# A two-layer transformer on one core: part products for layer 1's projections, and layer 2's scores as paired float32r products in bursts

## What is computed

```
x = x + attn0(layernorm(x));  x = x + ffn0(layernorm(x))
x = x + attn1(layernorm(x));  x = x + ffn1(layernorm(x))

attn0: q = (x @ w_q.T) in 16 heads;  k = x @ w_k.T;  v = x @ w_v.T     (one k and v for all heads)
       softmax(q k^T * softmax_scale) v, then @ w_out.T
ffn0:  x and the kernel rounded to fp8, product in float32, times the scales, to bfloat16, plus bias
attn1: q, k, v of all 16 heads from w_in;  scores = q k^T / 4 + slope_h * (key - query), -inf above the diagonal
       softmax, times v, then @ w_out.T
ffn1:  x @ W.T + b + x @ (up_aux @ lora_up @ lora_down @ down_aux).T
```

## Time and profile before

| | us |
|---|---|
| timed, median of 3 (lowest, highest) | 3888.25 (3883.73, 3889.77) |
| the profiled execution's own time | 3863.94 |
| its span | 3862.2 |
| PE busy in the span | 3636.8 (94%) |
| DVE busy | 2936.6 (76%) |
| ACT busy | 2471.1 (64%) |
| POOL busy | 1717.7 (44%) |

### The profile page before, as it was taken

One profiled execution on the slowest core, in us unless ns is written; L12 is line 12 of the kernel. 1 busy time (PEld: TensorE's weight loads), 2 busy tenths in 40 slices (PEclk: granted clock), 3 DMA queues, 4 the chain that ended last, 5 costly groups with the idle time before them and its releaser, 6 DMA issues. The chain is left out here.

```text
span 3862.2 us, 76074 instructions
## 1 busy us (share of the span) xinstructions
PE 3636.8 (94%) x25352; PEld 1854.5 (48%) x25352; DVE 2936.6 (76%) x8436; ACT 2471.1 (64%) x5347; POOL 1717.7 (44%) x1956
## 2 busy tenths in 40 slices
PE   5999999999999999998289999999999999999997
PEld 2344444444444444444145555555555555555554
DVE  4899999989998999995076776777767767777664
ACT  2777777777787777776055555555555555555554
POOL 1255555554555555554433343442433434424331
PEclk7999999999999999999599999999999999999999
DMA  3334333333333333331375755756657557566570
GB/s 70 73 77 87 80 90 76 83 79 91 76 82 88 85 84 81 83 74 37 72 120 89 127 104 96 122 105 105 115 93 124 106 94 125 104 103 116 94 122 23
DMA packets 323077, 352.93 MB, mean 91 GB/s; under 512 B 28101, under 2 KB 277371, under 8 KB 322683
## 3 DMA queue, kind: packets, MB, share of 16 engines
q1 hardware_dynamic: 320641, 347.01, 47.6%
q10 hardware_dynamic: 2048, 1.05, 0.1%
HBM read 221.08 MB, written 117.44 MB: 88 GB/s over the span
## 5 line engine op out<-in xcount | busy, mean ns | idle before, releaser
L666 DVE TENSOR_REDUCE maxima<-ps_vector 128x1 f32<-128x512 f32 x2048 | 1282.8, 682 | 162.0 <-PE ps_vector L435 155.6
L1559 DVE CUSTOM_DVE_ANT_0 ps_max<-ps_max,mask 128x128 f32<-128x128 f32 (+3 forms) x2048 | 987.2, 508 | 531.4 <-PE ps_max L1258 512.7
L1416 ACT ACTIVATE probs<-ps_exp 128x512 f32<-128x512 f32 (+3 forms) x2048 | 823.1, 441 | 783.6 <-PE ps_exp L1277 716.0
L564 ACT ACTIVATE probs<-ps_scalar 128x512 f32<-128x512 f32 x2048 | 1073.6, 604 | 155.6 <-PE ps_scalar L449 150.8
L435 PE MATMUL ps_vector<-k_op,q_op 48*128 48x512 f32 x2048 | 715.9, 446 | 48.1 <-DVE maxima L666 28.4
L449 PE MATMUL ps_scalar<-q_op,k_op 50*128 50x512 f32 x2048 | 708.1, 441 | 1.0 <-DVE o_rows L730 0.5
L1273 PE MATMUL ps_exp<-q_op,k_op 101*128 101x512 bf16 (+3 forms) x2048 | 614.3, 301 | 25.6 <-ACT probs L1416 18.0
L1258 PE MATMUL ps_max<-k_op,q_op 99*128 99x128 bf16 (+3 forms) x2048 | 619.4, 304 | 19.9 <-DMA k_op<-qk_parts 16.3
L435 PEld LDWEIGHTS ps_vector<-k_op,q_op 48*128 48x128 f32 x2048 | 333.3, 187 | 549.6 <-DVE maxima L666 394.8
L468 PE MATMUL ps_pv<-probs,v_op 128*32 128x512 f32 x4096 | 552.5, 606 | 0.0
L1704 POOL TENSOR_SCALAR neg_mean<-meanvar 128x4 f32<-128x4 f32 x64 | 12.5, 196 | 1092.0 <-issue 784.6
(11 more groups left out here) (127 smaller groups left out, 5186.0 us busy)
## 6 DMA issues: line engine op xcount, KB each, us to landing
q_op<-qk_parts SPq DMA_DIRECT2D x192, 256.0 KB, 5.9
qk_parts<-qparts SPq DMA_DIRECT2D x128, 384.0 KB, 3.2
q_op<-qk_parts SPq DMA_DIRECT2D x384, 128.0 KB, 6.4
k_op<-qk_parts SPq DMA_DIRECT2D x384, 128.0 KB, 6.9
qk_parts<-qparts SPq DMA_DIRECT2D x64, 512.0 KB, 4.2
xin<-in_x SPq DMA_DIRECT2D x32, 512.0 KB, 4.8
xres<-in_x SPq DMA_DIRECT2D x32, 512.0 KB, 4.6
x_mid<-xo SPq DMA_DIRECT2D x32, 512.0 KB, 3.2
```

What stands on the lines that cost most here:

```text
L564: act.activation(probs[:, quad % 2, at:at + S], ps_scalar[:, bank_of("scalar", "exp", p, 0, par), :], ACT.Exp).then_inc(ps_out["exp"], 1)
L666: dve.tensor_reduce(at, ps_vector[:, bank_of("vector", "max", k, d, par), :], AX.X, ALU.max).then_inc(ps_out["max"], 1)
L1416: act.activation(probs[:, quad % 2, at:at + nq], ps_exp[:, bank, 0:nq], ACT.Exp).then_inc(exp_done, 1)
L1559: ins = dve.tensor_tensor_reduce(row, row, mask[:, S - keys:S], 1.0, LOWEST, ALU.add, ALU.max, at)
```

## The change

In the first layer the projections for q, for keys with values and of the output become three products of float32r parts each, for both halves of the 256 columns (`TERMS`). The weights' parts are made once by DVE at the start. The parts of the operands are made by POOL in every body: `cut_x` twice and `cut_ont` twice, two instructions each. ACT writes the transposed columns to one staging tile first, which POOL then cuts. To fit, `xin`, `xo`, `kvf`, `kparts` and `o_rows` have one buffer instead of two. The plan is another one, and POOL and SP read their order from it too.

The second layer is written anew after the pattern of the first: q and k in two float32r parts (two POOL instructions), 51 and 53 rows high, heads 0 to 7 and 8 to 15 in the two halves of the partitions, operands in float32. Maximum tile and exponential tile of one pair have the same width, the widest first. The masks of a burst of pairs are issued ahead of it, into the banks of its exponentials (`put_mask`). The order comes from a plan, with 64 pairs in 21 bursts; three banks are for maxima and four for all the rest. A product with v waits for the tiles that it reads, not for the whole head group. The bias is added to x1 in place, and the output goes out one item after the body instead of two.

```
 PLAN_MQA = """
-PPP stat2:2:-2 qk:0:1
-PPP otr:2:-1 V
...
-PPPP otr:0:0 out:0:-1 ft:0:-2
-PPP V
-PPP split:0:1 stat1:1:2 out:1:-1
+PPP load_x:0:2 store_qk:0:1 qk:0:1
+PPP kv:0:1 split_qk:0:1
+PPP m:1:0 stat2:2:-2 split_kv:0:1 V
+PPP load_m:1:0 stat2:3:-2 norm2:0:-2 V stat1:0:2 over:0:-2 cut_ont:0:-1 V
...
+PPP ffn:0:-2 cut_x:1:2 split:0:1 otr:1:0 out:0:-1
+PPP m:0:1 load_q:1:1 load_m:0:1 V finish:0:-2 stat2:0:-1 ffn:1:-2 xt:0:2 stat2:1:-1 out:1:-1
+PPP xt:1:2 V store:0:-2
 first layer, PE's tasks:
                 elif kind == "qk":
-                    pe.wait_ge(ps_out["xt"], per["xt"] * (c + 1))
-                    for kt in range(KT):
-                        mm = pe.matmul(ps[:, :], w_qk[:, kt, k * P:(k + 1) * P], xT[:, cp, kt, :],
-                                       start=(kt == 0), stop=(kt == KT - 1))
+                    pe.wait_ge(x_cut, KT * (c + 1))
+                    for n, (kt, xp, wp) in enumerate(TERMS):
+                        mm = pe.matmul(ps[:, :], w_qk[:, wp, kt, k * P:(k + 1) * P], xT[:, xp, kt, :],
+                                       start=(n == 0), stop=(n == len(TERMS) - 1))
                 elif kind == "out":
-                    pe.wait_ge(ps_out["ont"], per["ont"] * (c + 1))
+                    pe.wait_ge(ont_cut, KT * (c + 1))
                     for t in (2 * k, 2 * k + 1):
-                        for kt in range(KT):
-                            mm = pe.matmul(ps[:, (t % 2) * D:(t % 2 + 1) * D], o_cols[:, kt, t * P:(t + 1) * P],
-                                           w_o[:, kt, :], start=(kt == 0), stop=(kt == KT - 1))
+                        for n, (kt, xp, wp) in enumerate(TERMS):
+                            mm = pe.matmul(ps[:, (t % 2) * D:(t % 2 + 1) * D], o_cols[:, xp, kt, t * P:(t + 1) * P],
+                                           w_o[:, wp, kt, :], start=(n == 0), stop=(n == len(TERMS) - 1))
 first layer, POOL:
+            def cut_x(c, k):
...
+                pool.wait_ge(ps_out["xt"], KT * c + k + 1)
+                split(x_cols[:, :], xT[:, :, k, :], x_step, KT * c + k).then_inc(x_cut, 1)
+
+            def cut_ont(c, k):
...
+                pool.wait_ge(ps_out["ont"], KT * c + k + 1)
+                split(o_half[:, :], o_cols[:, :, k, :], ont_step, KT * c + k).then_inc(ont_cut, 1)
 second layer, PE (removed and added):
-                pe.matmul(ps_max[:, bank, 0:keys], q_op[0:KA, cp * HEADS + h, i * P:(i + 1) * P],
-                          k_op[0:KA, kh, 0:keys], start=True, stop=True).then_inc(max_full, 1)
...
-                mm = pe.matmul(ps_exp[:, bank, 0:nq], k_op[0:KB, kh, T * P:(T + 1) * P],
-                               q_op[0:KB, par * HEADS + s, q0:q0 + nq], start=True, stop=not CAUSAL)
-                if CAUSAL:
-
-                    mm = pe.matmul(ps_exp[:, bank, 0:P], maskb[:, :], identb[:, :], start=False, stop=True)
+                h, T = divmod(k, NT)
+                i = NT - 1 - T
...
+                rows = slice(HALF_ROWS * unit, HALF_ROWS * unit + KA)
+                keys = (i + 1) * P
+                pe.matmul(ps_max[:, bank_of("max", "max", k, d, par), 0:keys],
+                          q_op[rows, cp, h % HALF, i * P:(i + 1) * P],
+                          k_op[rows, cp, h % HALF, 0:keys], start=True, stop=True).then_inc(ps_full["max"], 1)
...
+            def put_mask(p, b, par):
...
+                if held := held_before("rest", "exp", p, 0, b, par):
+                    pe.wait_ge(*held)
+                pe.matmul(ps_rest[:, bank_of("rest", "exp", p, 0, par), 0:P], maskb[:, :], identb[:, :],
+                          start=True, stop=False, skip_group_check=True)
...
+                pe.matmul(ps_rest[:, bank_of("rest", "exp", p, 0, par), 0:nq],
+                          k_op[at:at + KB, par, s % HALF, T * P:(T + 1) * P],
+                          q_op[at:at + KB, par, s % HALF, q0:q0 + nq],
+                          start=False, stop=True, skip_group_check=True).then_inc(ps_full["exp"], 1)
 second layer, POOL:
-                split(qf[:, k % 2, :], qparts[:, k % 2, :, :], qr[:, :], split_step, 3 * n).then_inc(qk_split, 1)
+                pool.tensor_scalar(parts[:, 0, :], qf[:, k % 2, :], 1.0, 0.0, ALU.mult, ALU.add).then_inc(split_step, 1)
+                pool.wait_ge(split_step, n + 1)
+                pool.tensor_tensor(parts[:, 1, :], qf[:, k % 2, :], parts[:, 0, :].bitcast(F32),
+                                   ALU.subtract).then_inc(qk_split, 1)
```

More of the change, by code:

```diff
@@ L32 @@
 M_ROWS = 2
+ALIBI = 3
 FP8_MIN_NORMAL = 2.0 ** -6
@@ L142, in layer_mqa @@
     FULL = NT * BANK
-    VECTOR_BANKS, SCALAR_BANKS = BANKS_MQA
+    MAX_BANKS, REST_BANKS = BANKS_MQA
+    TERMS = [(kt, xp, wp) for kt in range(KT) for xp, wp in ((0, 0), (0, 1), (1, 0))]
     x_tiles = x_in.rearrange("b (t p) d -> b p t d", p=P)
@@ new lines, in body @@
+            def body(b, par):
+                for kind, k, d in plan:
+                    if kind == "pair":
+                        max_tile(k, b, par)
+                    elif kind == "split":
+                        split_maxima(b + d, k)
+                    elif kind == "stat1":
+                        statistics(0, b + d, (par + d) % 2, k)
+                    elif kind == "stat2":
+                        statistics(1, b + d, (par + d) % 2, k)
+                    elif kind == "exponent":
+                        exponent(b + d)
+                    elif kind in BY_VECTOR:
+                        take_task(kind, k, d, b, par)
@@ L1841, in build @@
     })
-    layer(nc, 1, x_mid, out, w, shared | {
+    layer_causal(nc, x_mid, out, w, shared | {
         "w_qk": rows(w["wqk1T"]), "w_v": rows(w["wv1T"]), "w_o": rows(w["wo1T"]),
```

1787 lines of the change are left out of this document (794 added, 993 removed).

## The result

The changed kernel takes 3916.47 us (median of 12, 3891.6 to 3939.43) against 3883.59 for the kernel before (12 runs, 3861.08 to 3894.34): ratio 1.0089, 95% interval 1.0059 to 1.0119. I had forecast 3720. The profiled execution took 3891.6 us where my sum gave 3696; the 195.6 us between the two are what has to be found.

The account below looks back on a forecast made before the run. It took PE's streaming to bound the second layer and DVE nearly the first. Terms -144 (second layer), -22 (first) and -2 (starts) took 3864 to 3696 us profiled, times 1.0063 gives 3720; 8 in 10 range 3610 to 3850.

Parts of the forecast that it names:

- Nothing on the path: Second-layer transfers: half as many, twice the element size, same operand bytes, share 0.62; claimed to cost nothing.
- I let these cancel: Second layer: PE standing at bursts for banks against looser waits and a third bank; net nothing, 2 us an item either side.
- The price of the scores, 18.5 us: Second-layer scores an item: pairs 10.9, masks 3.8, going in and out of bursts 3.8, against 23.0 before; 4.5 us less.
- my 53.96: Forecast second-layer period in us an item, against 58.46 before.
- rival B: Second layer: switches of array shape eat 4.2 of the 4.5 us gained an item; timed 3854 us; chance 0.15.
- First layer, -0.7 us an item: Projections: half of PE's 1.6 us relief counted, -0.8, and 0.1 charged for the late load of x; -22 us in all.
- Rival C: First layer: the chain of cuts, additions, store and load of x on POOL and SP becomes the bound; 3977 us; chance 0.07.
- Rival D: Both layers: float32r products below 512 columns cost what 512 do, 0.24 us; timed 3925 us; chance 0.05.

Follow-up runs that it names:

- e5: Changed kernel, second layer, from the third item on: each load of queries and keys takes one head of eight (32 KB instead of 256); ratio to before 0.9842.
- e17: Changed kernel with those small loads in the second layer, ACT's exponentials and DVE's maxima there also over half the columns; ratio to the kernel before 0.9785.
- e4: Changed kernel, each second-layer mask put right before its own pair of scores instead of all of a burst ahead; ratio to the kernel before 1.0735.
- e13: Changed kernel with three one-input reductions for the first layer's maxima parts and a third, paced order of second-layer transfers; 3784.45 us, ratio to before 0.9749.
- e14: Same reductions and third order of transfers, but with the first layer of the kernel before; ratio to the kernel before 0.9818.
- e1: First layer of the kernel before with the second layer of the changed kernel; ratio to the kernel before 1.0012.
- e11: Changed kernel, first layer from the third item on: GpSimd's cuts of x and attention output take 8 columns instead of 512; ratio to before 1.0005.

## Why the prediction was wrong

The order of things in the forecast was right in part: pairs start together, DVE's waits for PE shrink, PE is relieved in the first layer. Point by point, in profiled time (195.6 us too low):

- **"Nothing on the path" and "I let these cancel"** are the steps that failed most. For the second layer I put the transfers at nothing, half as many and of the same bytes, and set missing banks against looser waits, at nothing too, with 2 us to either side. The first cost 2.07 (changed against e5: 1.44 of waits for the rows of the maxima behind the loads, at most 0.4 by the clock that stalls cost, the rest not found), the second at least 0.74 (e5 against e17): 2.8 us an item, 90 us. The share of the engines was the wrong row to read; what mattered was that a transfer of 16 KB on the path shares them with bursts of 3 MB, and that a load's time to landing would rise from 6.4 to 8.9 us.
- **The price of the scores, 18.5 us.** e17 stands 1.40 us above my 53.96: 45 us. By the medians of e17's trace (2000 to 3800 us) the pairs of a head cost 0.28, 0.17, 0.12 and 0.06, 10.1 us an item for my 10.9. But going in and out of a burst was priced from the first layer's bursts, which have no masks ahead of them. With masks there is one change more, and it all costs 0.275 a burst instead of 0.18: 2.0 us an item. The sum is 19.5, so 1.0 of the 1.40 is found. That was rival B, at half of the 4.2 us that it named; e4 shows the mechanism by itself.
- **First layer, -0.7 us an item.** The relief came near: e13 against e14 gives 0.93 with DVE free, where I counted 0.8. What I lacked is DVE's stall. I checked that GpSimd isn't full at 36 of 54 us and asked only what its four cuts delay, not whom they hold up. The stall behind all of GpSimd's work costs 2.06 us an item (55.06 in the changed kernel against 53.00 in e13), of which the kernel before had a part already (0.2 by its profile, 1.0 by the same layer in e1); the cuts themselves are 1.07 (e11). The profile had the hint: the maxima's high part at 182 ns median and 2128 at most in the kernel before, a row that I didn't look at. 2.06 - 0.21 - (0.93 - 0.70) = 1.62 us an item, the 52 us.
- **Rival C**, which I made the slow side, didn't happen: DVE's statistics of x waited for a load once, at the start (9.7 us). Rival D is refuted by the burst above. Two of the causes were in no rival: a queue and a port.
- **The base.** I took periods from one execution that was 0.5% faster than the median of the runs that followed, and its fast part was probably the layer that then looked worse.

What stays open: the 0.6% by which both new layers together are slower than their two shares; some 0.2 us an item of what the loads cost, and 0.4 of e17's distance; and whether a change of array shape costs its 0.09 us by a drain or by a load that stands bare.

## What to carry to other kernels

When transfers are merged or made wider, look for the small transfer that the critical engine waits for, and keep the time between its sending and its need free of large ones: pacing the loads with the same bytes took 1.2 us an item off (e13), and sending the rows up to 1.1 us earlier took nothing off. Before giving GpSimd work beside a DVE that is 90% busy, look at the maximum, not the median, of DVE's small instructions between SBUF tiles, and write them as reductions with one input where they are long. Price a burst with every change of array shape in it, its masks included, and check that a profiled base is a typical run before taking 1% from it.

## What the hardware showed that I had not expected

- The same work of DVE on 16 elements a partition took 834 ns (tensor_scalar) and 838 (scalar_tensor_tensor) at the median beside a busy GpSimd, up to 1727, and 158 as a tensor_reduce, never over 171. Each of the 90 long ones in the changed kernel ended 29 to 37 ns behind an instruction of GpSimd.
- 16 KB issued on ACT's queue were waited for until 14 us later, with 3 MB issued on SP's queue in the meantime; with small loads there (e5) no such wait was left.
- A stand of PE of 5 us took the granted clock to 0.60 over the 10 us from its start, in a layer that ran at 1.00 before the change.
- A float32r pair of 53 and 51 rows by 128 columns follows in 0.06 us, with stationary operands whose loads last 184 ns each: side by side and in a row the loads are hidden. Between two masks (e4) it costs 0.26.
